# Column sums of S as products with a column of ones on TensorE instead of additions on GpSimd

## The reference

```python
HW = einsum('bnf,fo->bno', layernorm(x), W)
A_norm = relu((A + A.T) * 0.5)
D = sum(A_norm, axis=1)                      # degree of each node
d_inv_sqrt = where(D > 0, D_safe ** (-0.5), 0.0)
L_norm = eye(N) - d_inv_sqrt[:, None] * A_norm * d_inv_sqrt[None, :]
x = x + relu(einsum('nm,bmo->bno', L_norm, HW))
x = x + moe(layernorm(x), ...)               # router, top 2 of 8 experts, gelu
```

## Time and profile before

| | us |
|---|---|
| median of 3 runs (lowest, highest) | 965.71 (964.76, 966.42) |
| profiled execution's own time | 967.4 |
| its span, first to last instruction | 965.7 |
| PE busy in the span | 900.4 (93%) |
| DVE busy | 645.8 (67%) |
| ACT busy | 517.5 (54%) |
| POOL busy | 310.2 (32%) |

### The profile page before, as it was taken

The page is one execution under the profiler, slowest core; times in us unless marked ns, Lnnn a source line. Parts: engine busy times, 40 slices in busy tenths (PEclk is TensorE's granted clock), DMA queues, the critical chain, the costliest instruction groups (busy, mean ns, idle before and its releaser), DMA issues.

```text
span 965.7 us, 15348 instructions
## 1 busy us (share of the span) xinstructions
PE 900.4 (93%) x4446; PEld 728.1 (75%) x4446; DVE 645.8 (67%) x1558; ACT 517.5 (54%) x899; POOL 310.2 (32%) x312
## 2 busy tenths in 40 slices
PE   4776799999999999999999688999999999999996
PEld 4774588888787888878888566777777777777774
DVE  3987543657877533333424376888888888888886
ACT  3665233243444312122121366888888888888885
POOL 0699234564666544463444400000000000000000
PEclk9997899999999999999999779999999999999999
DMA  9983265585766247866666653777777777777771
GB/s 285 330 239 119 98 240 218 210 293 170 251 219 203 81 158 265 299 254 237 252 233 250 245 194 141 265 265 265 265 265 265 265 265 265 264 264 266 265 265 44
DMA packets 93022, 222.98 MB, mean 231 GB/s; under 512 B 8856, under 2 KB 59568, under 8 KB 81072
## 3 DMA queue, kind: packets, MB, share of 16 engines
q1 hardware_dynamic: 86752, 211.59, 62.2%
q0 software_dynamic: 2560, 8.39, 2.2%
q10 hardware_dynamic: 3664, 2.43, 0.9%
HBM read 157.89 MB, written 64.49 MB: 230 GB/s over the span
## 4 chain that ended last, share of the span: by engine, by line
PE 82%; DVE 6%; POOL 4%; issue 3%; ACT 2%; DMA 2%; DVEq 0%; ACTq 0%; SPq 0%; POOLq 0%
PE bank L906 11%; PE bank L908 11%; PE bank L907 11%; PE bank L1272 7%; PE bank L1259 6%; PE bank L1261 6%; PE bank L1260 6%; PE bank L1274 6%; PE bank L1273 6%; POOL col_sum L543 2%; PE bank L854 2%; PE bank L330 2%; DVE y_lo L699 2%; PE bank L862 2%; PE bank L1280 2%
## 5 line engine op out<-in xcount | busy, mean ns | idle before, releaser
L1348 DVE TENSOR_TENSOR gated<-c_all,act_h 128x512 f32<-128x512 f32 x256 | 177.0, 692 | 63.6 <-ACT act_h L1310 58.5
L1310 ACT ACTIVATE act_h<-bank,b_sb 128x512 f32<-128x512 f32 x256 | 176.6, 690 | 77.8 <-PE bank L1261 74.9
L1353 DVE TENSOR_TENSOR g_lo<-gated,g_hi 128x512 fp32r<-128x512 f32 x256 | 175.5, 685 | 0.1
L1317 ACT ACTIVATE g_hi<-gated 128x512 fp32r<-128x512 f32 x256 | 159.0, 621 | 1.7 <-DVE gated L1348 1.7
L1244 POOL DMA_DIRECT2D out<-fin x32 | 24.3, 761 | 387.2 <-DVE fin L1361 382.1
L906 PE MATMUL bank<-y_hi,stage 128*128 128x512 f32 x256 | 111.7, 436 | 3.7 <-DVE y_lo L699 3.6
L1272 PE MATMUL bank<-g_hi,w_hi 128*128 128x512 f32 x256 | 107.8, 421 | 3.7 <-DVE g_lo L1353 3.6
L1259 PE MATMUL bank<-z_e,w_hi 128*128 128x512 f32 x256 | 105.3, 411 | 5.6 <-DMA z_e<-z_scratch 5.6
L988 POOL TENSOR_TENSOR rstd<-var_eps,neg_half 128x4 f32<-128x4 f32 x32 | 48.5, 1516 | 180.4 <-DVE var_eps L1025 179.9
L906 PE MATMUL bank<-y,stage 128*128 128x512 f32 x256 | 104.5, 408 | 0.0
L993 POOL TENSOR_SCALAR z<-x,mv,rstd 128x128 f32<-128x128 f32 x128 | 101.4, 805 | 3.4
(11 more groups left out here) (118 smaller groups left out, 1588.6 us busy)
## 6 DMA issues: line engine op xcount, KB each, us to landing
c_all<-c_scratch SPq DMA_DIRECT2D x64, 1024.0 KB, 8.0
s_scratch<-stage SPq DMA_DIRECT2D x14, 2048.0 KB, 8.4
stage<-s_scratch SPq DMA_DIRECT2D x14, 2048.0 KB, 8.0
z_e<-z_scratch SPq DMA_DIRECT2D x32, 512.0 KB, 6.9
z_scratch<-z_hl SPq DMA_DIRECT2D x31, 512.0 KB, 2.7
x_raw<-in_x SPq DMA_DIRECT2D x32, 256.0 KB, 7.4
x_res<-in_x SPq DMA_DIRECT2D x32, 256.0 KB, 7.3
r_e<-res_scratch SPq DMA_DIRECT2D x32, 256.0 KB, 2.7
```

What stands on the lines that cost most here:

```text
L1310: act.activation(v.act_h[e % R][:, :], ps_h[e % 2][:, :], ACT.Gelu, bias=v.b1_sb[:, e:e + 1]).then_inc(gelu_done, 1)
L1317: act.activation(v.g_hi[e % R][:, :], v.gated[e % R][:, :], ACT.Copy).then_inc(hi_done, 1)
L1348: dve.tensor_tensor(out=v.gated[e % R][:, :], in0=v.c_all[s][:, e, :], in1=v.act_h[e % R][:, :], op=ALU.mult).then_inc(gated_done, 1)
L1353: dve.tensor_tensor(out=v.g_lo[e % R][:, :], in0=v.gated[e % R][:, :], in1=v.g_hi[e % R][:, :].bitcast(FP32), op=ALU.subtract).then_inc(lo ...
```

## The change

The additions on POOL and the buffer `col_sum` go. When row j of S is through relu, PE multiplies each of its tiles left of the diagonal with the column of ones and accumulates in PSUM (`column_sums(j)`, j products), one step later in the loop. Each of the three parts of the degrees has a PSUM bank of its own (7, 2, 3), opened by one product with zeros. Since banks 2 and 3 are now in use, the turn groups of unit 0 take banks 4 and 5 of the projection, and wait for its last copies. POOL's queue holds only the inversions, the scaling of hw and the roots. `degrees(0)` moves on DVE from step 10 to step 8, `degrees(1)` from step 15 to step 13, and four of the 16 `y_high` and `y_low` move ahead of the last step.

```diff
-    ps_t = [v.banks[2], v.banks[3]]
+    ps_t = [v.banks[4], v.banks[5], v.banks[4], v.banks[5]] + [v.banks[2 + G % 2] for G in range(4, 64)]
...
     def turn_group(pe, u, g):
         n, G = column(u), st.groups_before[u] + g
+        if G == 0:
+            pe.wait_ge(v.pr.xt_copied, MB)
+        if G == 1:
+            pe.wait_ge(v.pr.hw_kept, MB)
+        if G in (4, 5):
+            pe.wait_ge(v.deg_step, v.deg_taken[G - 3])
         if G >= 2:
             pe.wait_ge(lo_made, ops_with[G - 2])
...
-    ps_d = v.banks[7]
+    ps_d = [v.banks[7], v.banks[2], v.banks[3]]
...
-        for r, j in enumerate(ROWS):
-            if 1 <= j <= MB - 2:
-                add_columns(j)
...
+        for first in range(0, MB, 4):
+            pr.invert(pool, range(first, first + 4))
+            if first == 8:
+                root(0)
+            for k in range(first, first + 4):
+                pr.scale_kept(pool, k)
+        root(1)
         root(2)
-        for k in range(8, MB):
-            pr.scale_kept(pool, k)
...
-        for m in range(MB - 1, -1, -1):
+            if r == 14:
+                for m in range(MB - 1, MB - 5, -1):
+                    y_high(m)
+        for m in range(MB - 5, -1, -1):
             y_high(m)
...
+        def column_sums(j):
+
+            pe.wait_ge(relued, until_row(j))
+            for p, (a, b) in enumerate(PARTS):
+                for k in range(a, min(b, j)):
+                    last = pe.matmul(ps_d[p][:, k:k + 1], s_tri[:, block(j, k), :], v.one_col[:, :], start=False,
+                                     stop=(j == a + 1))
             last.then_inc(col_done, 1)
...
+        for p, (a, b) in enumerate(PARTS):
+            pe.matmul(ps_d[p][:, a:b], ident[:, :], v.zeros[:, a:b], start=True, stop=False)
...
-            if j + 2 < MB:
-                column_sum(j + 2)
+            if j + 1 < MB:
+                column_sums(j + 1)
...
-        column_sum(1)
-        column_sum(0)
...
-            if r == 10:
+            if r == 8:
                 degrees(0)
                 st.diagonal(dve, 0)
...
-            if r == 15:
+            if r == 13:
                 degrees(1)
+            if r == 14:
+                for m in range(MB - 1, MB - 5, -1):
+                    y_low(m)
         degrees(2)
-        for m in range(MB - 1, 2, -1):
+        for m in range(MB - 5, 2, -1):
             y_low(m)
```

More of the change, by code:

```diff
@@ L110, in gnn_moe_kernel @@
         assert ends[0] <= y0_at + (MB // 2) * CW * 4 and ends[2] <= stage_at[1] + 2 * N * 4
-        setup_at = [ends[1]]
-        v.col_sum = sb("col_sum", [P, MB, P], FP32, setup_at)
+        setup_at = [ends[1] + 8 * 1024]
+        v.zeros = sb("zeros", [P, MB], FP32, setup_at)
         v.deg_low = sb("deg_low", [P, MB, Q], FP32, setup_at)
@@ L245, in project_program @@
     hw_done = sem("hw_done")
-    hw_kept = sem("hw_kept")
+    pr.hw_kept = hw_kept = sem("hw_kept")
     pr.hw_scaled = hw_scaled = sem("hw_scaled")
@@ L426, in turn_group @@
             i = m - Q * g
-            last = pe.transpose(ps_t[G % 2][:, i * P:(i + 1) * P], v.s_tri[:, block(n, m), :], v.ident[:, :])
+            last = pe.transpose(ps_t[G][:, i * P:(i + 1) * P], v.s_tri[:, block(n, m), :], v.ident[:, :])
         last.then_inc(s_turned, 1)
@@ L441, in low_group @@
         dve.tensor_tensor(out=v.stage[u % 2][:, 1, a:b, :].rearrange("p m f -> p (m f)"),
-                          in0=ps_t[G % 2][:, 0:(b - a) * P],
+                          in0=ps_t[G][:, 0:(b - a) * P],
                           in1=v.stage[u % 2][:, 0, a:b, :].rearrange("p m f -> p (m f)").bitcast(FP32),
@@ L495, in setup_stage @@
     v.deg_steps = STEPS * len(PARTS)
+    v.deg_taken = [STEPS * p + 2 for p in range(len(PARTS))]
     pr = v.pr = project_program(nc, sem, v)
@@ L526, in gpsimd @@
         pool.memset(v.neg_half[:, :], -0.5).then_inc(consts_made, 1)
-        pool.memset(v.col_sum[:, MB - 1, :], 0.0).then_inc(consts_made, 1)
+        pool.memset(v.zeros[:, :], 0.0).then_inc(consts_made, 1)
         for e in range(E):
@@ L532, in gpsimd @@
                            base=0, pattern=[[-1, P]], channel_multiplier=1).then_inc(consts_made, 1)
[L534 to L544, removed]
         def root(p):
@@ L550, in root @@
                                op=ALU.pow).then_inc(d_ready, 1)
-        for r, j in enumerate(ROWS):
-            if 1 <= j <= MB - 2:
-                add_columns(j)
[L555 to L558, removed]
-                root(0)
-            if r in (10, 11, 12, 13):
-                for k in range(2 * (r - 10), 2 * (r - 10) + 2):
-                    pr.scale_kept(pool, k)
-            if r == 14:
-                root(1)
+        for first in range(0, MB, 4):
+            pr.invert(pool, range(first, first + 4))
+            if first == 8:
+                root(0)
+            for k in range(first, first + 4):
+                pr.scale_kept(pool, k)
+        root(1)
         root(2)
-        for k in range(8, MB):
-            pr.scale_kept(pool, k)
     def scalar(act):
@@ L682, in degrees @@
             dve.wait_ge(deg_step, first + 1)
-            dve.wait_ge(col_done, MB - a)
-            dve.tensor_tensor(out=v.deg_raw[:, a:b], in0=ps_d[:, a:b], in1=v.deg_row[:, a:b], op=ALU.add).then_inc(deg_step, 1)
+            dve.wait_ge(col_done, MB - 1 - a)
+            dve.tensor_tensor(out=v.deg_raw[:, a:b], in0=ps_d[p][:, a:b], in1=v.deg_row[:, a:b], op=ALU.add).then_inc(deg_step, 1)
             dve.wait_ge(deg_step, first + 2)
```

3 lines of the change are left out of this document (1 added, 2 removed).

## The result

The changed kernel takes 969.86 us (median of 20 runs, 966.52 to 975.72), the kernel before, run beside it, 966.06 (20 runs, 962.93 to 969.51). The ratio is 1.0047 with a 95% interval of 1.0034 to 1.006: slower by 3.8 us, where 960.8 and faster were forecast. The profiled execution of the changed kernel took 973.43 us, with a span of 971.8 against 965.7 before.

The account below looks back on a forecast made before the run. The prediction took the setup's chain through POOL's additions and DVE up to 104.69, then PE, as the bound; 7.9 us lost, 9.9 gained, 2.95 from the clock gave 4.9 off 965.71: 960.8 us, range 954 to 969.

Parts of the forecast that it names:

- 51.6: step 11 turns at 75.7: Setup on PE: turns 12.0, products 22.3 and x blocks 17.3 us from 24.1 put step 11 at 75.7, before 68.84.
- products with one column leave PE at the low clock: Rival, setup: the clock falls behind product runs in steps 1 to 6, 1.7 us each, giving 971.0; chance 0.18.
- A product costs 0.22 in a run and 0.14 behind a turn: Price of a one-column product on PE: a run of n costs 0.22 n - 0.08 us.
- The rival with cheap products: Rival, setup on PE: products cost 0.14 us each, 8.4 less on PE, giving 953.4; chance 0.12.
- POOL paces nothing any more: Low parts of y on DVE: without POOL's additions each takes 0.66 us, all 16 10.6 instead of 17.0, gaining 6.4.
- PE is the bound of the setup: Steps 2 to 11: PE does not wait in between and becomes the setup's bound; 6.9 us are lost here.
- Step 11 to the third turn group: End of the setup: from step 11's turns at 75.7 to PE resuming at 102.7 or 102.8, 1.9 us earlier.
- The clock in the new pause: PE's wait of about 2 us before 102.75: the clock holds, 2.95 us more gained; bounds 0 and 2.95.
- The rival of the falling clock there: Rival, PE's pause before resuming: the clock falls, gain 1.9 us alone, giving 963.8; chance 0.18.
- The sum of 960.8: Whole kernel: 1.9 or 2.0 us gained, with the clock 4.9, counted against 965.71; chance 0.44.
- PE has no idle row after 104.69: Behind the setup PE never idles, so every microsecond by which 104.69 comes earlier is one of the whole time.
- the 9.9 us gained behind the second pair of low parts: End of setup: 24.6 us become 14.7; 6.4 from the low parts, 3.5 from last degrees no longer awaiting POOL's additions.

Follow-up runs that it names:

- e7_again: The changed kernel once more, unedited, for a second profile: 970.51 us, ratio 1.006 to the kernel before.
- e2_mixed: The changed kernel with its one-column products in steps 1 to 7 dealt out one to three at a time between turns and projections: 960.04 us, ratio 0.9932.
- e1_wide: The changed kernel with the same products moving 128 columns instead of one, output unchanged: 960.5 us, ratio 0.9948 to the kernel before.
- e6b_added: The kernel before with only runs of 15 down to 5 unread one-column products added in steps 1 to 11: 987.93 us, ratio 1.0236.
- e3_few: The changed kernel with 15 of its 120 products left, so its output is wrong: 951.89 us, ratio 0.9856 to the kernel before.
- e4_wide_late: e1_wide with the moves of degrees and of the high and low parts of y undone: 958.91 us, ratio 0.9938.
- e5_mixed_late: e2_mixed with the moves of degrees and of the high and low parts of y undone: 956.93 us, ratio 0.9929.

## Why the prediction was wrong

**The step that failed** is the third part's "51.6: step 11 turns at 75.7", which puts 105 turns, 105 products and twelve blocks of x at their full-clock prices with the clock at 1.00 from 20 to 80. PE was granted half the clock for 27.3 us of that stretch. 75.7 less 0.35 (step 1's turns came at 23.75) and plus 13.65 is 89.0; measured 87.97. What was at fault was not a price but the clock under all of them. It is the rival "products with one column leave PE at the low clock", which I gave 0.18: its mechanism, its side and its size (971.0 for six falls of 1.7 us; the profiled execution lost eight times 1.7 in five stretches, some of them two and three times as long) came true; e7_again, with only 3.4 us of work lost, shows that the size of a single execution could as well have been a quarter of it.

The evidence that I set against it was "from 20 to 60 and from 75 to 77, where such products stand in every step, the clock was 1.00". But there they stand in twos, with turns and projections before and behind; the change puts up to 15 in a row. In e2_mixed twos and threes left the clock at 1.00 from 20 to 85, so the row was right and told nothing of a run of 15. No row of the old trace could: its longest run of such products that I had is three. An operation in a pattern that the trace does not hold should have kept the odds near even, and not at 0.18.

**What held**, each by its own step:
- A product costs 0.22 in a run and 0.14 behind a turn. The rival with cheap products is out: 15 took 3.27 us at full clock.
- POOL paces nothing any more, and a low part of y takes 0.67 to 0.69 (forecast 0.66).
- PE is the bound of the setup: from step 2 to 11 its timeline has no idle row, and step 12 then waits 0.83 for its load.
- Step 11 to the third turn group: forecast 27.05 us (75.7 to 102.75), measured 27.27 (87.97 to 115.24) and 27.29 in e7_again.
- The clock in the new pause: PE waited 1.43 us before 115.24 and was at 1.00 behind it, so the 2.95 us of the old low stretch were indeed saved. The rival of the falling clock there is out; PE's waits at this place were 0.36 to 1.43 us in all the traces without GpSimd's additions, not the 2 us forecast, and the clock held in each.
- The sum of 960.8 came out in e1_wide, 960.5, where the clock holds in the setup, but only in part by its own terms: 3.1 us of the gain are there at the end of the graph stage, where the forecast has 4.9, and 4.2 came at the hand-over to the experts. That part of the agreement is luck.

From PE's resumption to the end: it came 10.55 us later than before; the low stretch behind it that is gone gives back 3 of that, which leaves 7.6, and the last product of the graph stage starts 7.7 later (550.08 against 542.36). The span grew by 6.1. The other 1.6 were gained behind that, where the changed kernel's clock was 0.86 over 50 us and the old one's 0.76. I did not test it; the same 50 us had 0.76 in e2_mixed, 0.86 in e7_again and e6b_added and 0.90 in e1_wide, e3_few, e4_wide_late and e5_mixed_late; from that last product to the end the nine traces take from 418.5 to 423.3 us. This varies by more than the whole measured effect of 3.8 us, and a profiled span has to be read with it. It also bounds a sentence of the prediction, that PE has no idle row after 104.69 and every microsecond there is one of the whole time: the kernel before waits 5.62 us for a load at 548.37, and the rows that the prediction read end long before.

One part of the argument was weaker than it read. Of the 9.9 us gained behind the second pair of low parts I gave 3.5 to the last degrees. The trace has those microseconds, but e4 and e5 show that moving degrees and low parts ahead brings none of them. That POOL leaving the queue of S does is what remains: from step 11 to the resumption the kernel before takes 35.85 us and e6b_added 36.4, both with POOL's additions and late scaling, and e4_wide_late 26.0. The new banks were not undone by themselves.

## What to carry to other kernels

When work is moved to TensorE, price it twice: once by the duration of its instructions, and once by what it may do to the clock of everything around it. A long run of matmuls that move one column each (ten to fifteen here) can halve the granted clock for microseconds although PE is never idle; look for the longest such run in the old trace before trusting its quiet stretches, and deal such products between wider ones, or widen them, which here left a product at 0.22 us. And measure such a kernel over many executions: one trace showed five falls, another two. When a variant lands on the forecast, check where in the span its gain lies before calling the forecast right.

## What the runs showed of the hardware

- The granted clock was at 1.2 GHz for 3.4 to 10 us at a time with PE busy throughout; it fell within a run of 10 to 15 one-column float32 products or up to 1.3 us behind its end, seven times in the two traces of the changed kernel. The Trainium skill's page TensorE: Matmul & The Clock Gate, section HAM oscillation, knows the fall as the consequence of PE standing idle; here 38.87 of 40 us were busy at a mean of 0.79, so the measurement goes beyond it.
- The same products with 128 moving columns took the same 0.22 us and kept 2.4 GHz. Why, no run here shows; only that widening them, or spacing them, was enough.
- Before PE's resumption, pauses of 1.41 and 1.43 us left the clock at 1.00 (e7_again and the changed kernel), where the old trace's fall at 66 stands behind one of 1.66. Neither length is a limit: the falls at 79.8 in the old trace and at 77.5 in e5_mixed_late stand behind waits of under 1 us beside one-column products.
